# Fused attention on one core: the order of TensorE's work inside a key tile

## The chip, the cores and the metric

The kernel runs on one core of a Trainium2 chip. The metric is the device time of one execution, in microseconds (us). The core has five engines that work side by side: TensorE (PE, with its weight loads PEld), VectorE (DVE), ScalarE (ACT), GpSimd (POOL) and SyncE (SP), which issues DMA transfers. Each runs its own list of instructions in order, and they wait for one another by semaphores.

## The reference

Two transformer layers for 4 batches of 1024 tokens with 128 channels. The change touches the attention of the second layer alone. It has a dense part with 16 heads of 8 channels, and a sparse part with one head of 64 channels that keeps the 204 largest weights of each row. (The sizes written in its first line are not the input's; the token count here is 1024.)

```python
def _L1_attn_ref(src, in_proj_w, in_proj_b, out_proj_w, out_proj_b, Qp_w, Qp_b, Kp_w, Kp_b, Vp_w, Vp_b, lam, ...):
    B, S, D, H, R, DFF = (4, 128, 128, 16, 64, 512)
...
    scores = jnp.einsum('bhqd,bhkd->bhqk', q, k) / math.sqrt(dh)
    attn = jax.nn.softmax(scores, axis=-1)
    ctx = jnp.einsum('bhqk,bhkd->bhqd', attn, v)
    ctx = ctx.transpose(0, 2, 1, 3).reshape(b, s, d)
    dense_output = ctx @ out_proj_w.T + out_proj_b
    Q = src @ Qp_w.T + Qp_b
    K = src @ Kp_w.T + Kp_b
    V = src @ Vp_w.T + Vp_b
    QK = jnp.einsum('bqr,bkr->bqk', Q, K) / math.sqrt(R)
    aw = jax.nn.softmax(QK, axis=-1)
    kk = max(1, int(s * 0.2))
    topv, topi = jax.lax.top_k(aw, kk)
...
    sparse_attn = sparse_attn / (jnp.sum(sparse_attn, axis=-1, keepdims=True) + 1e-09)
    sparse_output = jnp.einsum('bqk,bkd->bqd', sparse_attn, V)
    sig = jax.nn.sigmoid(lam)
    fused = sig * dense_output + (1.0 - sig) * sparse_output
```

## The kernel before

`attend` (from line 2247) computes both parts. It walks over 4 batches, and in each over 4 groups (`GROUPS`), so 16 groups. The dense part of a group is four heads; the sparse part of a group is two tiles of 128 rows (t = 0 and 1). A group has 32 steps (`STEPS`): 8 key tiles of 128 keys, and in each key tile two pairs of heads times two halves of the 1024 queries (`c`). "Key tile" below means four steps, n = 4k to 4k + 3.

Each step n is a score on TensorE (`score`, line 2532): two matmuls, one for each head of the pair, into `scores_ps[n % 2]`. ScalarE then takes the exponential into `probs` (line 2505). There are only two score buffers, so score n waits until exponential n - 2 is done (line 2529). One step's output is 128 x 1024 numbers.

The value products (`values`, line 2549) multiply the exponentials of the key tile before by its values into `pv_ps`: four matmuls of 32 columns for each half c. They are accumulated over the 8 key tiles, and the last key tile's are made in the next group's first steps. Then VectorE copies `pv_ps` to `pv` (`keep_pv`, line 2666, counted by `pv_kept`), and the first product of the next group (`kt == 0`, issued at n = 5) waits for that copy (line 2547).

The side work goes through one buffer, `misc`, whose uses follow one another: `misc_made` counts what TensorE has made, `misc_used` what was taken out. For each group these are: the two sparse scores of this group (`sparse_scores`, line 2569), which VectorE takes out (`keep_scores`, line 2670); and for the previous group the turned output (`turn_out`, 2580), the turned sparse weights (`turn_weights`, 2589), which ScalarE copies out (`keep_turned`, 2482), and the product with the sparse values (`sparse_values`, 2598), for t = 0 and 1. In the kernel before, turn_out, turn_weights and sparse_values are issued in halves of four 128-column blocks, each behind a score of its own.

`PE_AT` and `ACT_AT` say behind which step each piece of side work is issued. On TensorE: sparse scores behind 0 and 4, then the halves in pairs behind 7 and 8, 11 and 12, 15 and 16, 19 and 20, 23 and 24. On ScalarE: `rows_exp` (line 2478, the sparse rows' exponential) behind exponentials 14 and 22, `keep_turned` behind 13 and 21.

VectorE runs one long list for a group (`body`, line 2806): the first sparse score out, the copy of `pv`, the second sparse score out, then the search for the cut of each row, the weights and the outputs. At its end (line 2781) `w_ready` lets TensorE turn the group's weights. At the end of the stage (`end`, line 2648) the last group's side work is done with nothing beside it: eight transposes, both value products in a row, eight transposes.

## Time and profile before

| what | us |
|---|---|
| median of 3 runs | 1391.15 |
| lowest and highest run | 1388.97, 1391.48 |
| the profiled execution | 1388.52 |
| its span in the profile | 1386.8 |
| of that, `attend`, first score to last group's end | 473.8 to 1118.7 |

Busy shares over the span are TensorE 91%, VectorE 75%, ScalarE 66%, GpSimd 40%. They are means over stages with different limits. A row of a group of instructions gives how often it ran, its busy time, the mean length of one, and how long its engine stood idle just before it and for whom. A row of the timeline gives the start, the length, the engine, the line, the operation with its tiles, and how many were merged into it. A duration reaches from the start to the last result, so on ScalarE and TensorE the next instruction can start before the one before has ended; what counts for the pace is the distance of the starts.

### The profile page before, as it was taken

How to read it: one execution, taken by the hardware profiler on the slowest of the kernel's cores; microseconds unless marked ns; L12 is line 12 of the kernel's file. 1: busy time of each engine (PE TensorE's matmuls, PEld its weight loads, DVE VectorE, ACT ScalarE, POOL GpSimd, SP SyncE). 2: the span in 40 equal slices, each digit the busy share in tenths (PEclk: the TensorE clock that was granted, in tenths of full speed). 3: DMA queues.
4: the chain of work that ended last, by engine and by line, in shares of the span. 5: the costliest groups of instructions: out<-in, count | busy, mean ns of one | idle time of the engine just before them, and what ended most of it. 6: DMA issues, size and time to landing. Idle time of an engine off the chain costs nothing. (4 is left out here: it accounts for less than half of the span.)

```text
span 1386.8 us, 28727 instructions
## 1 busy us (share of the span) xinstructions
PE 1266.7 (91%) x9145; PEld 810.6 (58%) x9146; DVE 1041.6 (75%) x2727; ACT 917.3 (66%) x1321; POOL 557.6 (40%) x696
## 2 busy tenths in 40 slices
PE   6999759999986689999999999998999989998999
PEld 4877759999954224443333344333344366878898
DVE  5656267688778688888888788887898858786654
ACT  4565523333356488898888888887888838774232
POOL 6337978867779310222222022222112200488700
PEclk9999779999988899999999999999999989999999
DMA  8980013332335731222221212222122023011211
GB/s 262 224 56 22 31 55 106 98 87 77 93 100 186 200 48 33 40 37 44 41 43 32 35 32 37 44 42 45 21 32 41 3 88 101 19 58 58 70 36 32
DMA packets 100385, 93.96 MB, mean 68 GB/s; under 512 B 20034, under 2 KB 84000, under 8 KB 100256
## 3 DMA queue, kind: packets, MB, share of 16 engines
q1 hardware_dynamic: 92960, 77.51, 25.7%
q0 software_dynamic: 6144, 12.73, 3.0%
q10 hardware_dynamic: 1152, 2.10, 0.5%
q8 instruction: 69, 1.13, 0.4%
q14 instruction: 60, 0.49, 0.2%
HBM read 50.40 MB, written 41.89 MB: 67 GB/s over the span
## 5 line engine op out<-in xcount | busy, mean ns | idle before, releaser
L2505 ACT ACTIVATE probs<-scores_ps 128x1024 f32<-128x1024 f32 x512 | 507.0, 1027 | 89.5 <-PE scores_ps L2532 84.9
L2532 PE MATMUL scores_ps<-q_pack,k_pack 64*128 64x512 f32 x1024 | 245.7, 492 | 37.0 <-ACT probs L2505 21.0
L2532 PEld LDWEIGHTS scores_ps<-q_pack,k_pack 64*128 64x128 f32 x1024 | 96.2, 184 | 310.4 <-issue 163.6
L2549 PE MATMUL pv_ps<-probs,v_pad 128*32 128x512 f32 x2048 | 275.5, 611 | 0.0
L2426 POOL TENSOR_TENSOR squares<-sparse_scores 128x512 f32<-128x512 f32 x32 | 41.0, 1280 | 476.9 <-DVE sparse_scores L2670 476.7
L1447 ACT ACTIVATE hidden_experts<-pre_experts 128x512 f32<-128x512 f32 x94 | 59.3, 631 | 109.5 <-DVE pre_experts L1381 83.1
L2742 DVE TENSOR_SCALAR_CACHE_REDUCE junk<-sparse_scores,at 128x1024 f32<-128x1024 f32 x96 | 122.8, 1279 | 3.4
L1469 PE MATMUL up_ps_experts<-x_t_experts,up_weights_now_experts 128*128 128x128 f32 x752 | 105.2, 284 | 5.5 <-DVE up_weights_now_experts L1376 3.9
L1469 PEld LDWEIGHTS up_ps_experts<-x_t_experts,up_weights_now_experts 128*128 128x128 f32 x752 | 92.6, 194 | 11.0 <-DVE up_weights_now_experts L1376 8.0
L1476 PE MATMUL down_ps_experts<-weights_t,hidden_experts 128*128 x736 | 97.2, 275 | 0.0
L3340 POOL DMA_INDIRECT expert_rows_dram<-expert_input_tail,send_to_tail x64 | 62.5, 977 | 79.5 <-DVE send_to_tail L3468 61.0
L1476 PEld LDWEIGHTS down_ps_experts<-weights_t,hidden_experts 128*128 128x128 f32 x736 | 89.5, 192 | 0.0
L3669 ACT ACTIVATE hidden_tail<-up_ps_tail,weights_t 128x160 f32<-128x160 f32 x128 | 40.9, 393 | 67.0 <-PE up_ps_tail L3808 66.1
L2549 PEld LDWEIGHTS pv_ps<-probs,v_pad 128*32 128x32 f32 x2048 | 40.6, 108 | 64.3 <-issue 62.2
L168 POOL DMA_INDIRECT expert_rows_dram<-expert_input,pick x64 | 64.6, 1009 | 31.0 <-issue 22.9
L1381 DVE TENSOR_TENSOR pre_experts<-up_ps_experts,weights_t 128x512 f32<-128x512 f32 x94 | 64.2, 683 | 16.1 <-PE up_ps_experts L1469 15.2
L2598 PE MATMUL misc_ps<-sparse_v,sparse_w_t 128*128 (+1 forms) x480 | 69.5, 288 | 0.0
L2598 PEld LDWEIGHTS misc_ps<-sparse_v,sparse_w_t 128*128 128x128 f32 x480 | 58.1, 191 | 14.3 <-issue 14.3
L1376 DVE COPY up_weights_now_experts<-weights_t 128x512 f32 x96 | 62.6, 654 | 1.6 <-PEq L462 1.4
L2670 DVE TENSOR_SCALAR_CACHE_REDUCE sparse_scores<-misc_ps 128x1024 f32<-128x1024 f32 x32 | 39.2, 1225 | 26.6 <-PE misc_ps L2569 17.1
L3840 PE MATMUL out_ps_tail<-gated_out_pieces_tail,place_tail 128*128 128x128 bf16 x960 | 56.7, 219 | 0.0
L3840 PEld LDWEIGHTS out_ps_tail<-gated_out_pieces_tail,place_tail 128*128 128x128 bf16 x960 | 55.2, 98 | 0.5
(420 smaller groups left out, 2545.6 us busy)
## 6 DMA issues: line engine op xcount, KB each, us to landing
q_pack<-q_pieces_dram SPq DMA_DIRECT2D x128, 64.0 KB
k_pack<-k_pieces_dram SPq DMA_DIRECT2D x128, 64.0 KB
expert_rows_dram<-zeros SPq DMA_DIRECT2D x1, 6400.0 KB, 22.8
x_rows_experts<-expert_rows_dram SPq DMA_DIRECT2D x25, 256.0 KB
expert_rows_dram<-y_rows_experts SPq DMA_DIRECT2D x46, 128.0 KB, 1.8
q_pieces_dram<-q_pieces_prep SPq DMA_DIRECT2D x8, 512.0 KB, 4.1
k_pieces_dram<-k_pieces_prep SPq DMA_DIRECT2D x8, 512.0 KB, 4.5
expert_rows_dram<-zeros SPq DMA_DIRECT2D x1, 2640.0 KB, 40.2
```

The lines of the kernel that those rows point to most:

```text
L168: pool.indirect_dma_start(self.rows, bass.IndirectOffsetOnAxis(ap=g.pick0[:, b, k, n : n + 1], axis=0), self.h[:, b * NT + n, :], None).th ...
L1376: dve.tensor_copy(up_now[:, k % UNROLL], up_w(e)).then_inc(up_here, 1)
L1381: dve.tensor_tensor(pre[:, k % 2], up_ps[k % 2][:], up_bias(e).unsqueeze(2).to_broadcast([P, FC, P]), ALU.add).then_inc(pre_ready, 1)
L1469: ins = pe.matmul(up_ps[k % 2][:, c, :], up_now[:, k % UNROLL, c, :], x_t[:, k % UNROLL, :], start=True, stop=True)
L1476: ins = pe.matmul(down_ps[k % 2][:, 0:C], hidden[:, k % 2, c, :], down_w(e, c), start=(c == 0), stop=(c == FC - 1))
L2505: act.activation(probs[:, kt % 2, 2 * pair : 2 * pair + 2, c * 512 : c * 512 + 512], scores_ps[n % 2][:].rearrange("p (h t) -> p h t", h=2 ...
L2532: ins = pe.matmul(scores_ps[n % 2][:, head * 512 : head * 512 + 512], k_pack[group % 2][rows, pair, kt * P : kt * P + P].bitcast(F32R), q_ ...
L2549: ins = pe.matmul(pv_ps[32 * j : 32 * j + 32, c, :], v_pad[:, group % 2, kt, j, :], probs[:, kt % 2, j, c * 512 : c * 512 + 512], start=(k ...
L2598: ins = pe.matmul(misc[:, 0:C], w_t[:, n, :], f.sparse_v[:, bass.ds(b * NT + n, 1), :].rearrange("p n c -> p (n c)"), start=(n == 0), stop ...
L2742: step(dve.tensor_scalar(junk[:], s[:, t, :], at[:, t : t + 1], None, ALU.is_ge, ALU.add, accum_out=count[:, t : t + 1]))
L3340: pool.indirect_dma_start(expert_rows.rows, bass.IndirectOffsetOnAxis(ap=send_to[:, b, k, n : n + 1], axis=0), n3[:, b % 3, n, :], None).t ...
L3840: ins = pe.matmul(out_ps[h][:, i * C : i * C + C], place[:, (b * SLOT_TILES + t) % PLACES, n * P : n * P + P], pieces[:, (b * MIX_PARTS + ...
```

## The change

The order inside a key tile is another, and so are the places of the side work. Before, TensorE issued: score, (half a side piece), score, value product 0, score, value product 1, score, (half a side piece). Now it issues: score, score, both value products, score, score, one whole side piece. The whole pieces stand behind steps 3, 7, 11, 15, 19, 23 and 27 of a group. ScalarE's `rows_exp` moves behind exponentials 18 and 26 and `keep_turned` behind 17 and 25. The instructions of each kind, their sizes, their buffers and the lists of VectorE, GpSimd and SyncE stay as they are.

```diff
-PE_AT = (0, 4, 7, 8, 11, 12, 15, 16, 19, 20, 23, 24)
-ACT_AT = (14, 22, 13, 21)
+PE_AT = (3, 7, 11, 15, 19, 23, 27)
+ACT_AT = (18, 26, 17, 25)
...
-                def halves(part):
-                    return range(part * HALF, part * HALF + HALF)
-
-                def turn_out(b, group, number, part):
-                    if part == 0:
-                        free(number)
-                        pe.wait_ge(pv_kept, b * GROUPS + group + 1)
-                    for n in halves(part):
+                def turn_out(b, group, number):
+                    free(number)
+                    pe.wait_ge(pv_kept, b * GROUPS + group + 1)
+                    for n in range(NT):
                         ins = pe.transpose(misc[:, n * P : n * P + P], pv[:, n * P : n * P + P], g.ident[:])
-                    if part == 1:
-                        ins.then_inc(misc_made, 1)
+                    ins.then_inc(misc_made, 1)
...
-                            for part in range(2):
-                                side |= {
-                                    PE_AT[2 + part]: lambda part=part: turn_out(*prev, use(*prev, 2), part),
-                                    PE_AT[4 + part]: lambda part=part: turn_weights(*prev, 0, use(*prev, 3), part),
-                                    PE_AT[6 + part]: lambda part=part: sparse_values(*prev, 0, part),
-                                    PE_AT[8 + part]: lambda part=part: turn_weights(*prev, 1, use(*prev, 5), part),
-                                    PE_AT[10 + part]: lambda part=part: sparse_values(*prev, 1, part),
-                                }
+                            side |= {
+                                PE_AT[2]: lambda: turn_out(*prev, use(*prev, 2)),
+                                PE_AT[3]: lambda: turn_weights(*prev, 0, use(*prev, 3)),
+                                PE_AT[4]: lambda: sparse_values(*prev, 0),
+                                PE_AT[5]: lambda: turn_weights(*prev, 1, use(*prev, 5)),
+                                PE_AT[6]: lambda: sparse_values(*prev, 1),
+                            }
                         for n in range(STEPS):
                             score(b, group, n)
 
-                            if n % 4 in (1, 2):
-                                if n >= 4:
-                                    values(b, group, n // 4 - 1, n % 4 - 1)
-                                elif not alone:
-                                    values(*prev, NT - 1, n % 4 - 1)
+                            if n % 4 == 1:
+                                for c in range(2):
+                                    if n >= 4:
+                                        values(b, group, n // 4 - 1, c)
+                                    elif not alone:
+                                        values(*prev, NT - 1, c)
                             if n in side:
                                 side[n]()
```

`turn_weights` and `sparse_values` change in the same way as `turn_out`, and so does the call of `turn_out` in `end`.

In the order's rows, x counts matmuls: a score is x2, one half's value product x4. Lines of the kernel before are named L2532 (score), L2549 (value product), L2569 (sparse score), L2589 (turned weights); in the changed kernel these are L2531, L2548, L2568 and L2582. TensorE, the start of a group before: the first row is the last score of the group before and score 0, the last row the second sparse score:

```order
-L2532 MATMUL scores_ps<-q_pack,k_pack 128x512 x4
-L2569 MATMUL misc_ps<-sparse_keys_now,sparse_q_tile 128x512 x2
-L2532 MATMUL scores_ps<-q_pack,k_pack 128x512 x2
-L2549 MATMUL pv_ps<-probs,v_pad 32x512 x4
-L2532 MATMUL scores_ps<-q_pack,k_pack 128x512 x2
-L2549 MATMUL pv_ps<-probs,v_pad 32x512 x4
-L2532 MATMUL scores_ps<-q_pack,k_pack 128x512 x4
-L2569 MATMUL misc_ps<-sparse_keys_now,sparse_q_tile 128x512 x2
```

and now, from scores 2 and 3 on:

```order
+L2531 MATMUL scores_ps<-q_pack,k_pack 128x512 x4
+L2568 MATMUL misc_ps<-sparse_keys_now,sparse_q_tile 128x512 x2
+L2531 MATMUL scores_ps<-q_pack,k_pack 128x512 x4
+L2548 MATMUL pv_ps<-probs,v_pad 32x512 x8
+L2531 MATMUL scores_ps<-q_pack,k_pack 128x512 x4
+L2568 MATMUL misc_ps<-sparse_keys_now,sparse_q_tile 128x512 x2
+L2531 MATMUL scores_ps<-q_pack,k_pack 128x512 x4
+L2548 MATMUL pv_ps<-probs,v_pad 32x512 x8
```

Before, four scores and both halves of the last group's product stood between the two sparse scores, and the group's own first product (behind score 5) came only after the second one. Now the last group's product is made ahead of the first row shown, the first sparse score comes behind score 3, and only scores 4 and 5 lie between it and the group's own first product (the x8 row), which waits for the copy of `pv`.

TensorE, a key tile with turned weights, before:

```order
-L2549 MATMUL pv_ps<-probs,v_pad 32x512 x4
-L2532 MATMUL scores_ps<-q_pack,k_pack 128x512 x2
-L2549 MATMUL pv_ps<-probs,v_pad 32x512 x4
-L2532 MATMUL scores_ps<-q_pack,k_pack 128x512 x2
-L2589 MATMUL misc_ps<-ident,sparse_exp 128x128 x4
-L2532 MATMUL scores_ps<-q_pack,k_pack 128x512 x2
-L2589 MATMUL misc_ps<-ident,sparse_exp 128x128 x4
-L2532 MATMUL scores_ps<-q_pack,k_pack 128x512 x2
```

and now:

```order
+L2548 MATMUL pv_ps<-probs,v_pad 32x512 x8
+L2531 MATMUL scores_ps<-q_pack,k_pack 128x512 x4
+L2582 MATMUL misc_ps<-ident,sparse_exp 128x128 x8
+L2531 MATMUL scores_ps<-q_pack,k_pack 128x512 x4
+L2548 MATMUL pv_ps<-probs,v_pad 32x512 x8
```

A score was followed by something else four times in such a tile, and is twice now; the scores stand in pairs.

## Rows read from the trace of the kernel before

**Rows 1.** The page's part 5: busy, mean ns, idle before, and releasers.

```profile
L2505 ACT ACTIVATE probs<-scores_ps 128x1024 f32<-128x1024 f32 x512 | 507.0, 1027 | 89.5 <-PE scores_ps L2532 84.9
L2532 PE MATMUL scores_ps<-q_pack,k_pack 64*128 64x512 f32 x1024 | 245.7, 492 | 37.0 <-ACT probs L2505 21.0 <-PEq L1847 10.0 <-issue 5.3
```

**Rows 2.** Busy time by engine (count) in the last group's window; PEclk, DMA, GB/s.

```profile
1078.05:1117.85 39.80, 38.89 (x258) 15.65 (x256) 34.13 (x78) 35.26 (x38) 9.35 (x9) 1.00 0.02 5
```

**Rows 3.** Timeline of TensorE's weight loads, last group: start us, length us, engine, work.

```profile
1088.82 0.18 PEld L2532 LDWEIGHTS scores_ps<-q_pack,k_pack 64*128 64x128 f32 x2 [0.17 <-issue]
1089.24 0.16 PEld L2549 LDWEIGHTS pv_ps<-probs,v_pad 128*32 128x32 f32 x8 [0.24 <-issue]
1090.24 0.19 PEld L2532 LDWEIGHTS scores_ps<-q_pack,k_pack 64*128 64x128 f32 x2 [0.84 <-ACT probs L2505]
...
1092.09 0.42 PEld L2589 LDWEIGHTS misc_ps<-ident,sparse_exp 128*128 128x128 f32 x4 [0.24 <-issue]
1092.68 0.19 PEld L2532 LDWEIGHTS scores_ps<-q_pack,k_pack 64*128 64x128 f32 x2 [0.17 <-issue]
...
1093.70 0.18 PEld L2532 LDWEIGHTS scores_ps<-q_pack,k_pack 64*128 64x128 f32 x2 [0.17 <-issue]
...
1096.97 0.97 PEld L2598 LDWEIGHTS misc_ps<-sparse_v,sparse_w_t 128*128 128x128 f32 x8 [0.24 <-issue]
1098.06 0.19 PEld L2532 LDWEIGHTS scores_ps<-q_pack,k_pack 64*128 64x128 f32 x2
...
1113.16 0.38 PEld L2532 LDWEIGHTS scores_ps<-q_pack,k_pack 64*128 64x128 f32 x4 [0.84 <-issue]
1114.78 0.19 PEld L2532 LDWEIGHTS scores_ps<-q_pack,k_pack 64*128 64x128 f32 x2 [1.24 <-ACT probs L2505]
...
1117.63 0.19 PEld L2532 LDWEIGHTS scores_ps<-q_pack,k_pack 64*128 64x128 f32 x2 [0.84 <-issue]
1118.71 0.86 PEld L2637 LDWEIGHTS scores_ps<-ident,sparse_exp 128*128 128x128 f32 x8 [0.89 <-ACT probs L2505]
1119.73 0.16 PEld L2549 LDWEIGHTS pv_ps<-probs,v_pad 128*32 128x32 f32 x8 [0.17 <-issue]
...
1121.59 0.86 PEld L2637 LDWEIGHTS scores_ps<-ident,sparse_exp 128*128 128x128 f32 x8 [0.84 <-issue]
```

**Rows 4.** Timeline of ScalarE in the same stretch.

```profile
1096.96 1.16 ACT L2478 ACTIVATE sparse_exp<-sparse_scores,minus_row_max 128x1024 f32<-128x1024 f32 x1
...
1098.10 3.04 ACT L2505 ACTIVATE probs<-scores_ps 128x1024 f32<-128x1024 f32 x3
...
1113.71 2.85 ACT L2505 ACTIVATE probs<-scores_ps 128x1024 f32<-128x1024 f32 x3 [0.41 <-PE scores_ps L2532]
...
1118.17 1.02 ACT L2505 ACTIVATE probs<-scores_ps 128x1024 f32<-128x1024 f32 x1 [0.40 <-PE scores_ps L2532]
```

**Rows 5.** Timeline of all engines at the start of the last group.

```profile
1078.23 0.41 PEld L2569 LDWEIGHTS misc_ps<-sparse_keys_now,sparse_q_tile 64*128 64x128 f32 x4
...
1079.51 1.23 DVE L2670 TENSOR_SCALAR_CACHE_REDUCE sparse_scores<-misc_ps 128x1024 f32<-128x1024 f32 x1 [0.97 <-PE misc_ps L2569]
...
1080.90 0.15 DVE L2673 TENSOR_SCALAR minus_row_max<-row_max 128x1 f32<-128x1 f32 x1 [0.16 <-DVE sparse_scores L2670]
...
1082.48 1.23 DVE L2666 COPY pv<-pv_ps 128x1024 f32<-128x1024 f32 x1 [1.42 <-PE pv_ps L2549]
...
1083.98 1.22 DVE L2670 TENSOR_SCALAR_CACHE_REDUCE sparse_scores<-misc_ps 128x1024 f32<-128x1024 f32 x1 [0.28 <-PE misc_ps L2569]
```

**Rows 6.** Windows in the first group (columns of rows 2), then TensorE's timeline there.

```profile
490.80:494.20 3.40, 1.90 (x16) 0.69 (x14) 3.26 (x7) 3.31 (x5) 0.00 (x0) 1.00 0.68 96
501.10:504.50 3.40, 1.89 (x18) 0.72 (x14) 3.30 (x5) 3.40 (x6) 0.00 (x0) 1.00 0.05 16
504.50:507.90 3.40, 3.40 (x18) 0.49 (x10) 3.29 (x6) 1.84 (x2) 0.00 (x0) 0.50 0.03 7
...
503.55 0.49 PE L2532 MATMUL scores_ps<-q_pack,k_pack 64*128 64x512 f32 x2 [1.51 <-ACT probs L2505]
```

More of the change, by code:

```diff
@@ L2256, in attend @@
     LAST = GROUPS - 1
-    HALF = NT // 2
     LOADS = 2 * (2 * PIECES * PIECES + 1)
@@ L2570, in sparse_scores, with turn_weights, sparse_values @@
                     ins.then_inc(misc_made, 1)
[L2572 to L2597 removed]
+                def turn_out(b, group, number):
+                    free(number)
+                    pe.wait_ge(pv_kept, b * GROUPS + group + 1)
+                    for n in range(NT):
+                        ins = pe.transpose(misc[:, n * P : n * P + P], pv[:, n * P : n * P + P], g.ident[:])
+                    ins.then_inc(misc_made, 1)
+                def turn_weights(b, group, t, number):
+                    free(number)
+                    pe.wait_ge(w_ready, b * GROUPS + group + 1)
+                    for n in range(NT):
+                        ins = pe.transpose(misc[:, n * P : n * P + P], e[:, t, n * P : n * P + P], g.ident[:])
+                    ins.then_inc(misc_made, 1)
+                def sparse_values(b, group, t):
+                    pe.wait_ge(w_t_ready, (b * GROUPS + group) * 2 + t + 1)
+                    for n in range(NT):
                         ins = pe.matmul(
@@ L2604, in sparse_values @@
                         )
-                    if part == 1:
-                        ins.then_inc(misc_made, 1)
+                    ins.then_inc(misc_made, 1)
                 def body(b, first):
@@ L2652, in end @@
                     last_weights(b, 1)
-                    for part in range(2):
-                        turn_out(b, LAST, last_use(2), part)
+                    turn_out(b, LAST, last_use(2))
                     for t in range(2):
```

11 lines of the change are left out of this document (removed).

## The prediction, as it was put on record before the changed kernel ran

> **What bounds the kernel now.** I read the page first, then a window over one group of the fused attention, then the timelines of the weight loads (they mark where TensorE's next piece begins) and of ScalarE in that group. The change touches only `attend`, which runs from 473.8 to 1118.7 us, 16 groups. ScalarE is idle for 89.5 us before its 512 exponentials, nearly always for a score, and TensorE is idle for only 37.0 us before its scores [rows 1]. One group takes 39.8 us with TensorE busy for 38.9 of them, VectorE for 34.1 and ScalarE for 35.3 [rows 2]. So TensorE paces it. In the weight loads the reader is to see a fixed pattern: score to value product 0.42 us, value product to score 1.00, four transposes to score 0.59 [rows 3]. A key tile with half a transpose piece behind two of its scores takes 2 x (0.42 + 1.00) + 2 x (0.42 + 0.59) = 4.86 us and nothing in it waits: from 1088.82 to 1093.70. The sparse product piece has 1.09 per half (1096.97 to 1098.06).
>
> Two chains run behind that, and both have slack now. First, the scores alternate between two buffers, so score n waits for exponential n-2: an exponential that starts at 1113.71 frees the score load at 1114.78, 1.07 us later [rows 3, 4]. A score that loads at 1117.63 starts its exponential at 1118.17, 0.54 us later [rows 3, 4]; three exponentials in a row take 2.85 us where one takes 1.02, so they start 0.91 apart [rows 4]. Second, VectorE copies a finished `pv_ps` out (L2666) only after it has taken the first sparse score (L2670) [rows 5], and the first value product of the next group waits for that copy.
>
> **The change: what it takes off TensorE.** The loads of two scores in a row are 0.19 apart (0.38 us for two scores' loads from 1113.16), against 0.42 when a product follows. Two value products in a row stand once in the trace, in the end of the stage: 1119.73 to 1121.59, 1.86 us, against 2.00 for two halves. Eight transposes in a row take 1.02 (1118.71 to 1119.73), against 1.18 [rows 3]. So a tile needs 2 x (0.19 + 0.42) + 1.86 + 1.02 = 4.10 us of TensorE in place of 4.86. That is the gain. For the sparse product whole, no row stands in this order; it is between 1.94 (twice the 0.97 us of a half's eight loads) and 2.18 (two halves as they stand) [rows 3], and I take 2.0. It is hidden in either case.
>
> **What it puts on the two-buffer chain.** Count from the load of the second score of a tile, s1, at 0. The products start at 0.42 and s2 loads at 0.42 + 1.86 = 2.28. ScalarE started the exponential before s0 at -1.07 (that is what lets s1 load at 0), those of s0 and s1 at -0.16 and 0.75, and is dry from 1.78. Exponential s2 starts at 2.28 + 0.54 = 2.82, exponential s3 at 3.73, and the next tile's s1, which needs the buffer of s3, loads at 3.73 + 1.07 = 4.80. The side piece (from 2.89 to 3.91, or 4.89 for the sparse product) lies wholly beside this. So the period is 4.80 us for a tile with transposes, with nothing or with sparse scores: TensorE's saving is spent waiting. Where ScalarE also does `rows_exp` between the two exponentials (n = 18 and 26), its start-to-start pitch of 1.14 (1096.96 to 1098.10) [rows 4] comes on top: 5.94. `keep_turned` behind n = 17 and 25 is a pass of the shape of an exponential and falls into the dry time before s2: nothing. Group: 6 x 4.80 + 2 x 5.94 = 40.7 us.
>
> **What it puts on the copy of pv.** The first sparse scores move from behind n = 0 to behind n = 3. They load at 2.47 + 0.19 = 2.66. VectorE takes them 1.28 later (1078.23 to 1079.51), its next small operation starts 1.39 after that (1080.90), and I add 0.1 to reach the copy: 5.43 [rows 5]. The copy takes 1.23, and I add 0.1 for the release: 6.76. Today the copy starts late for another reason (it waits for the products behind n = 2, 1082.48) but is followed by a score, sparse scores and a score before n = 5 needs it; after the change only two scores lie between, and the products behind n = 5 would start at 4.80 + 0.42 = 5.22. So they wait 1.5 us, in order, with every later score behind them. The ends for this wait: 0, if VectorE got to the copy before the sparse scores, which the code's order excludes, and 2.0. Group: 40.7 + 1.5 = 42.2, which is 2.4 more than 39.8. The other moved pieces keep their distance: turned output, weights and their keepers all move three or four steps, like VectorE's stream that feeds them. GpSimd's squares and the DMA queue wait for VectorE and for score counts and are not near the path.
>
> **End, start, loops.** The stage ends when VectorE has finished its stream: from its second sparse score at 1083.98 [rows 5] to the transposes at 1118.71 [rows 3] are 34.7 us. Now that score comes 10.3 after s1 of tile 0 (products 6.76, s2 8.62, sparse scores 8.99, plus 1.28), so the last group lasts 0.9 + 10.3 + 34.7 = 45.9 from its first score, in place of 1118.71 - 1078.05 = 40.7: +5.2. For the first group, which has no previous one to work off, I take +1.5 (between 0 and 3: same period, no wait for pv). At the two loop turns the scores lose 5.3 us to issue [rows 1]; about 1 us of each falls into the new wait of the first scores: -2.
>
> Sum without the clock: 14 x 2.4 + 5.2 + 1.5 - 2 = +38.
>
> **The clock.** From 501.1 to 504.5 TensorE was busy 1.89 of 3.40 us, and the granted clock was 0.50 in the next stretch, the 1.2 GHz level; after 490.8 with 1.90 it stayed full [rows 6]. After the change, from the end of the first sparse scores to the products behind n = 5 (about 3.8 to 6.76), TensorE does two scores, 0.8 to 1.0 us in 3.0. That is less busy than the stretch before that fall. I expect a fall in most groups, 13 of 15. At the low level the double product that follows would need up to 1.86 more and the scores some tenths; where the clock falls later, part of the cost lies in waits. Between 0.9 and 2, I take 1.6 per fall: +21. The Trainium skill, "TensorE: Matmul & The Clock Gate", section "HAM oscillation — how this bites in real kernels", says that only idle gaps well above any here have to be avoided. By it no fall would come and the time would be rival B's. The row at 501.1 speaks against it, as its longest gap was 1.51 us [rows 6].
>
> Total +59 us. Profiled execution: 1388.5 + 59 = 1447.5; the median of the runs shown is 2.6 above that execution, so 1450 us.
>
> **Rivals.** B: everything as above, but the clock stays: 1391.15 + 38 = 1429. For it: the fall depends on alignment, and 490.8 had no fall at 1.90 busy. C: the wait for pv doesn't arise or is covered and only the two-buffer chain acts: 14 x 0.9 + 3.7 + 1.5 - 2 = +16, so 1407. Against it: the order of VectorE's list. D, the other side: the exponentials are fed in time, because the pair of products needs less than its one sighting in the end stage, so that the saving on TensorE counts. It decides at a tile period of 4.97 with no wait for pv (39.8 / 8); if it holds fully, TensorE needs 8 x (1.22 + 1.86) and some 9.3 of side work, 34 us a group, and VectorE's stream is next, 1.5 + 1.3 + 34.7 = 37.5: 15 x 2.3 = 34 less, 1357. Against it: the products must stream between s1 and s2 while ScalarE holds at most two scores. E: the clock falls twice in a group, also at the tile without a side piece, where TensorE needs only 3.1 of 4.80: another 13 x 1.6, so 1471. That the change doesn't do what it says is excluded by the order: pairs of scores, eight products, whole pieces.
>
> **Numbers.** Forecast A 0.53, B 0.20, E 0.09, C 0.09, D 0.06, unplaced 0.03. Range 1424 to 1466: A and B with the bounds of the fall's price. A measurement of this kernel tells about 0.2% from no change. Faster by over 0.2%: 0.06; within: 0.03; slower: 0.91.
>
> **What would show it.** Right: groups of about 42 to 44 us; score loads in pairs 0.19 apart; a period of 4.80 in quiet tiles and 5.94 in the two with `rows_exp`; ScalarE idle for a score about 1.0 us before every n = 2 mod 4; TensorE waiting for L2666's copy, 1.5 us a group; a granted clock of 0.50 for a stretch in most groups. Wrong: TensorE without waits for exponentials behind the pairs (D), no wait for the copy (C), clock 1.00 throughout (B). My weakest term is the clock, then the double product, seen once.

## The result

The changed kernel is slower. Its median is 1464.49 us (4 runs, 1460.33 to 1470.27) against 1391.32 us of the kernel before (4 runs, 1388.97 to 1391.54): a ratio of 1.054, with a 95% interval of 1.0515 to 1.0565. The forecast was 1450 us, 59 us more than before. The medians differ by 73. The direction came as forecast and the size was too small. The mechanism came as forecast in the plain groups, and not in the first group and at the loop turns.

The profiled execution is the longest of its four (1470.27 us, span 1468.5). Against the one of before it is 81.7 us longer, so the accounts below, which are made from these two, hold some 8 us more than the medians do.

The lines that answer to [rows 1], from the page's part 5 of the changed kernel (busy, mean ns, idle before, and releasers):

```profile
L2504 ACT ACTIVATE probs<-scores_ps 128x1024 f32<-128x1024 f32 x512 | 486.4, 1028 | 178.4 <-PE scores_ps L2531 174.6
L2531 PE MATMUL scores_ps<-q_pack,k_pack 64*128 64x512 f32 x1024 | 226.6, 481 | 87.2 <-ACT probs L2504 72.7
L2548 PE MATMUL pv_ps<-probs,v_pad 128*32 128x512 f32 x2048 | 277.2, 663 | 28.2 <-DVE pv L2654 25.4
L2658 DVE TENSOR_SCALAR_CACHE_REDUCE sparse_scores<-misc_ps 128x1024 f32<-128x1024 f32 x32 | 39.2, 1225 | 117.1 <-PE misc_ps L2568 103.8
```

The same list shows VectorE idle before the sparse scores for 103.8 us, since TensorE now makes them later. ScalarE's idle time for a score went from 84.9 to 174.6 us, and TensorE's idle time for an exponential from 21.0 to 72.7. Each now waits for the other, in turns. A third wait is new: 25.4 us in which TensorE's products wait for VectorE's copy of `pv`.

Busy time by engine (PE, PEld, DVE, ACT, POOL), granted clock, DMA share and GB/s of two groups, as in [rows 2]: first one in which the clock fell, then one in which it stayed.

```profile
1104.11:1148.11 44.00, 38.23 (x256) 16.25 (x257) 34.51 (x81) 34.25 (x39) 7.34 (x9) 0.96 0.23 34
880.73:923.08 42.35, 36.60 (x256) 15.82 (x256) 35.06 (x82) 34.24 (x39) 7.34 (x9) 1.00 0.24 35
```

At full clock TensorE is busy for 36.6 us in a group, 2.3 less than the 38.9 of before. So the work on TensorE did shrink as meant. But the group takes 42.35 us in place of 39.80.

**A quiet tile.** The weight loads of TensorE, as in [rows 3], in a key tile with turned weights behind it and in the one that follows:

```profile
897.66 0.19 PEld L2531 LDWEIGHTS scores_ps<-q_pack,k_pack 64*128 64x128 f32 x2 [0.66 <-ACT probs L2504]
898.09 0.16 PEld L2548 LDWEIGHTS pv_ps<-probs,v_pad 128*32 128x32 f32 x8 [0.24 <-issue]
...
899.94 0.30 PEld L2531 LDWEIGHTS scores_ps<-q_pack,k_pack 64*128 64x128 f32 x4 [0.84 <-ACT probs L2504]
900.60 0.85 PEld L2582 LDWEIGHTS misc_ps<-ident,sparse_exp 128*128 128x128 f32 x8 [0.36 <-issue]
901.62 0.19 PEld L2531 LDWEIGHTS scores_ps<-q_pack,k_pack 64*128 64x128 f32 x2 [0.17 <-ACT probs L2504]
902.47 0.19 PEld L2531 LDWEIGHTS scores_ps<-q_pack,k_pack 64*128 64x128 f32 x2 [0.66 <-ACT probs L2504]
...
908.42 0.18 PEld L2531 LDWEIGHTS scores_ps<-q_pack,k_pack 64*128 64x128 f32 x2 [0.83 <-ACT probs L2504]
```

From the second score of one tile to that of the next are 4.81 us (897.66 to 902.47), and 5.95 to the next (908.42), in whose middle `rows_exp` stands. The double product holds the next pair of scores for 1.85 us after its own load at 898.09. ScalarE in the same tile:

```profile
895.67 3.77 ACT L2504 ACTIVATE probs<-scores_ps 128x1024 f32<-128x1024 f32 x4 [1.05 <-PE scores_ps L2531]
900.48 1.02 ACT L2504 ACTIVATE probs<-scores_ps 128x1024 f32<-128x1024 f32 x1 [1.04 <-PE scores_ps L2531]
```

It does four exponentials in a row, 3.77 us, then has nothing for 1.04 us. That is the chain of the prediction: two buffers hold two scores, and the third can't come before both products are through.

**The copy of pv.** All engines at the start of a group, as in [rows 5]:

```profile
884.27 0.43 PEld L2568 LDWEIGHTS misc_ps<-sparse_keys_now,sparse_q_tile 64*128 64x128 f32 x4
...
885.58 1.23 DVE L2658 TENSOR_SCALAR_CACHE_REDUCE sparse_scores<-misc_ps 128x1024 f32<-128x1024 f32 x1 [0.94 <-PE misc_ps L2568]
...
886.46 0.19 PEld L2531 LDWEIGHTS scores_ps<-q_pack,k_pack 64*128 64x128 f32 x2 [0.73 <-ACT probs L2504]
...
887.08 1.23 DVE L2654 COPY pv<-pv_ps 128x1024 f32<-128x1024 f32 x1
...
888.46 1.92 PE L2548 MATMUL pv_ps<-probs,v_pad 128*32 128x512 f32 x16 [1.49 <-DVE pv L2654]
```

The products could have started 0.42 us after the load of score 5 at 886.46. They start at 888.46. VectorE first took the late sparse score out (885.58), then copied `pv` (887.08), and TensorE stood for 1.49 us.

**The clock.** Windows in the same columns, first two in the first group, which answer to [rows 6], then two around the start of another plain group (at 742.08), then three around the start of the last but one group (at 1104.11), and TensorE's timeline there:

```profile
501.30:504.70 3.40, 1.01 (x6) 0.37 (x4) 3.33 (x6) 3.35 (x5) 0.00 (x0) 1.00 0.53 65
504.70:508.10 3.40, 3.40 (x18) 0.59 (x16) 3.30 (x5) 1.54 (x2) 0.00 (x0) 0.50 0.03 9
740.20:743.60 3.40, 2.10 (x16) 0.83 (x16) 3.26 (x7) 2.60 (x3) 0.00 (x0) 1.00 0.26 61
743.60:747.00 3.40, 3.40 (x18) 0.57 (x10) 1.68 (x7) 1.17 (x2) 0.00 (x0) 0.50 0.51 69
1102.00:1105.40 3.40, 2.10 (x16) 0.67 (x8) 3.29 (x6) 2.37 (x3) 0.00 (x0) 1.00 0.26 65
1108.80:1112.20 3.40, 1.46 (x10) 0.56 (x12) 2.58 (x4) 2.82 (x4) 1.85 (x2) 1.00 0.55 65
1112.20:1115.60 3.40, 3.40 (x18) 1.03 (x12) 0.00 (x0) 0.00 (x0) 1.98 (x4) 0.51 0.57 83
```

```profile
1109.84 0.50 PE L2531 MATMUL scores_ps<-q_pack,k_pack 64*128 64x512 f32 x2 [0.42 <-ACT probs L2504]
1111.84 3.29 PE L2548 MATMUL pv_ps<-probs,v_pad 128*32 128x512 f32 x16 [1.49 <-DVE pv L2654]
1115.05 1.00 PE L2531 MATMUL scores_ps<-q_pack,k_pack 64*128 64x512 f32 x4
...
1118.28 1.92 PE L2548 MATMUL pv_ps<-probs,v_pad 128*32 128x512 f32 x16
```

In the stretch that holds the wait for `pv` TensorE was busy for 1.46 of 3.40 us; the granted clock of the next stretch is 0.51, the 1.2 GHz level. The double product that falls into it takes 3.29 us, and the next one, at full clock, 1.92. The falls come at two places. In five of the ten plain groups the fall comes at this wait for `pv`. In three it comes earlier, 1.4 to 1.6 us after the group's first score, behind a tile without a side piece: the stretch before 743.60 has 2.10 us of work and no gap above 0.9 us, and the next one ran at 0.50. The stretch from 1102.00 has 2.10 us of work too, and no fall behind it.

From the first score of `attend` to its last, TensorE's clock fell 20 times, where it had fallen 3 times before. One more fall, at 1194.2, comes between the last score and the end of the last group.

**Where the 81.7 us are.** The length of a group is from its first score's load to that of the next group.

| stretch | before | after | difference | forecast |
|---|---|---|---|---|
| up to the first score of `attend` | 473.8 | 475.4 | +1.6 | 0 |
| first group | 38.9 | 48.6 | +9.7 | +1.5 |
| ten plain groups | 397.7 | 436.5 | +38.9 | +38 to +40 |
| four groups beside the two loop turns | 167.7 | 187.6 | +19.9 | some +14 |
| last group, to the transposes | 40.7 | 47.6 | +6.9 | +5.2 |
| after `attend` | 268.1 | 272.8 | +4.7 | 0 |

Of the ten plain groups, two took 42.20 and 42.36 us without a fall of the clock, and eight took 43.93 to 44.04 with one. The eight tiles of a group took 4.82, 7.19, 4.89, 4.82, 5.78, 4.99, 5.78 and 4.92 us (first score to first score, medians of the ten plain groups).

### The profile page after: what moved, and what is told of

Same layout as the page of the kernel before. It is cut to its first block and busy times, and to the rows that moved or that the text cites. A ratio compares the mean times of both kernels' runs of the same rounds, so it can differ in the third digit from the quotient of the medians.

```text
span 1468.5 us, 28727 instructions
## 1 busy us (share of the span) xinstructions
PE 1264.3 (86%) x9145; PEld 819.3 (56%) x9146; DVE 1044.2 (71%) x2727; ACT 901.0 (61%) x1321; POOL 551.8 (38%) x696
## 5 line engine op out<-in xcount | busy, mean ns | idle before, releaser
L2504 ACT ACTIVATE probs<-scores_ps 128x1024 f32<-128x1024 f32 x512 | 486.4, 1028 | 178.4 <-PE scores_ps L2531 174.6
L2531 PE MATMUL scores_ps<-q_pack,k_pack 64*128 64x512 f32 x1024 | 226.6, 481 | 87.2 <-ACT probs L2504 72.7
L2548 PE MATMUL pv_ps<-probs,v_pad 128*32 128x512 f32 x2048 | 277.2, 663 | 28.2 <-DVE pv L2654 25.4
L2531 PEld LDWEIGHTS scores_ps<-q_pack,k_pack 64*128 64x128 f32 x1024 | 88.3, 189 | 296.0 <-ACT probs L2504 235.7
L2425 POOL TENSOR_TENSOR squares<-sparse_scores 128x512 f32<-128x512 f32 x32 | 40.8, 1274 | 552.5 <-DVE sparse_scores L2658 552.5
L2548 PEld LDWEIGHTS pv_ps<-probs,v_pad 128*32 128x32 f32 x2048 | 58.3, 115 | 148.6 <-issue 125.6
L2658 DVE TENSOR_SCALAR_CACHE_REDUCE sparse_scores<-misc_ps 128x1024 f32<-128x1024 f32 x32 | 39.2, 1225 | 117.1 <-PE misc_ps L2568 103.8
L3657 ACT ACTIVATE hidden_tail<-up_ps_tail,weights_t 128x160 f32<-128x160 f32 x128 | 40.8, 393 | 69.8 <-PE up_ps_tail L3796 68.6
L2588 PE MATMUL misc_ps<-sparse_v,sparse_w_t 128*128 (+1 forms) x480 | 61.5, 281 | 0.0
```

What stands on the lines that cost most here:

```text
L2504: act.activation(probs[:, kt % 2, 2 * pair : 2 * pair + 2, c * 512 : c * 512 + 512], scores_ps[n % 2][:].rearrange("p (h t) -> p h t", h=2 ...
L2531: ins = pe.matmul(scores_ps[n % 2][:, head * 512 : head * 512 + 512], k_pack[group % 2][rows, pair, kt * P : kt * P + P].bitcast(F32R), q_ ...
L2548: ins = pe.matmul(pv_ps[32 * j : 32 * j + 32, c, :], v_pad[:, group % 2, kt, j, :], probs[:, kt % 2, j, c * 512 : c * 512 + 512], start=(k ...
L2588: ins = pe.matmul(misc[:, 0:C], w_t[:, n, :], f.sparse_v[:, bass.ds(b * NT + n, 1), :].rearrange("p n c -> p (n c)"), start=(n == 0), stop ...
```

## The experiments

In the table "plain group" is the length of most groups of the stage, and "falls" counts, in the one profiled execution, how often the granted clock fell to its lower level between the first and the last score of `attend`. The ratios are to the kernel before as it ran in the same session. Its medians there were 1389.2 to 1391.3, so a plain difference of two medians can be some 2 us off.

| kernel | median us | ratio to before (95%) | plain group | falls |
|---|---|---|---|---|
| before | 1391.3 | | 39.8 | 3 |
| changed | 1464.5 | 1.054 (1.0515 to 1.0565) | 42.2 or 44.0 | 20 |
| e3: before, products paired | 1423.3 | 1.0242 (1.0225 to 1.0259) | 41.4 | 6 |
| e2: changed, products apart | 1442.3 | 1.0389 (1.0371 to 1.0406) | 41.8 | 8 |
| e1: changed, sparse scores early | 1428.9 | 1.028 (1.0256 to 1.0304) | 41.2 | 8 |
| e12: changed, copy of pv first | 1427.1 | 1.0242 (1.0207 to 1.0278) | 40.8 | 6 |
| e5: changed, scores repeated | 1447.1 | 1.0414 (1.0389 to 1.044) | 42.4 | 4 |
| e6: e5, more in the first group | 1445.4 | 1.0396 (1.038 to 1.0411) | 42.4 | 3 |
| e13: changed, no loops | 1448.6 | 1.0425 (1.0387 to 1.0463) | 42.3 or 43.9 | 12 |
| e9: changed, `rows_exp` later | 1480.0 | 1.0647 (1.0632 to 1.0663) | 43.0 to 45.2 | 18 |
| e4: whole side pieces | 1385.9 | 0.9978 (0.9966 to 0.9991) | 39.2 to 39.6 | 3 |
| e7: one side piece in each tile | 1414.7 | 1.0161 (1.0136 to 1.0187) | 40.2 to 42.4 | 7 |
| e10: e7, `rows_exp` behind 18 and 23 | 1387.0 | 0.9972 (0.9956 to 0.9988) | 39.6 | 2 |
| e11: e7, `rows_exp` behind 14 and 22 | 1378.8 | 0.9914 (0.9892 to 0.9936) | 39.0 | 3 |
| e14: e11, no loops | 1368.2 | 0.9843 (0.9818 to 0.9869) | 39.0 | 0 |

### Pairing alone

e3 is the kernel before with one edit: both value products stand behind the second score.

```diff
-                            if n % 4 in (1, 2):
-                                if n >= 4:
-                                    values(b, group, n // 4 - 1, n % 4 - 1)
-                                elif not alone:
-                                    values(*prev, NT - 1, n % 4 - 1)
+                            if n % 4 == 1:
+                                for c in range(2):
+                                    if n >= 4:
+                                        values(b, group, n // 4 - 1, c)
+                                    elif not alone:
+                                        values(*prev, NT - 1, c)
```

> The kernel before with one edit: both value products behind n = 1 mod 4. Side work stays in halves and sparse scores behind 0 and 4. Theory: the two-buffer chain alone acts. Tiles take 4.8 to 4.9 us (before: 4.47 to 5.4, with only the slow ones bound by TensorE), those with rows_exp 5.9, a group about 41.4 in place of 39.8, total about 1417 us, with few falls of the clock. Rival (TensorE's pace counts, and the pairing saves it 0.14 on the products and 0.23 on the scores of a tile): about 8 x 0.37 x 16 = 47 us less, down to 1345 us, or VectorE's bound at 1357 us.

Measured: 1423.34 us, 34 us more than before in the same session (1389.17). A plain group without a fall takes 41.43, with tiles of 4.8 to 5.1 and two of 5.81. The chain of the two buffers holds, and needs nothing else of the change. The rival that pairing saves time falls.

e2 is the other way round, the changed kernel with the products apart again (the same lines, + and - exchanged).

> The changed kernel with its value products apart again, behind n = 1 and 2 mod 4; sparse scores and whole side pieces stay where the change put them. Theory: the last score of a tile now loads 2.84 us after the second, the next tile's second one at 2.84 + 0.54 + 1.07 = 4.45 in place of 4.80, so quiet tiles take 4.45 to 4.5 us and those with rows_exp about 5.7. The wait for the copy of pv grows to about 2.2, as the double product no longer covers part of it. Group about 40.4 without a fall, 42 with one; total about 1435 us. Rival (no two-buffer chain, the wait for pv and the clock make the whole loss): tiles as before at best, loss at least as large, 1465 us or more.

Measured: 1442.27 us. The direction is right, but the group is 1.4 us longer than expected: 41.77. From second score to second score a quiet tile takes 4.46 or 4.47. Eight of these are 35.8. Of the 6.0 above, 2.2 come with the wait for `pv`, which is still there (the step of the product behind score 5 takes 3.66 us where others take 1.42 to 1.53), and twice 1.8 with the tiles in which `rows_exp` and a whole side piece stand beside each other (6.31 each).

### The copy of pv

Two experiments take that wait away, on different engines. e1 moves the two sparse scores on TensorE:

```diff
-PE_AT = (3, 7, 11, 15, 19, 23, 27)
+PE_AT = (0, 4, 11, 15, 19, 23, 27)
```

> The changed kernel with its two sparse scores back behind steps 0 and 4; pairs, double products and all other whole pieces stay. My theory (three terms: two-buffer chain, wait for the copy of pv, clock): the wait before the products of step 5 goes, since VectorE can copy pv about 1.5 us before they are due. The sparse scores now stand between the two scores of a pair and cost about 0.35 us each: 40.7 + 0.7 = 41.4 us a group in place of the 42.2 of the groups of the changed kernel without a fall. If the falls of the clock come from that wait they mostly go too, and the time is about 1425 us; if they come from the whole pattern they stay at 1.8 a group, 1450 us. Rival (the double products alone make the time, the wait for pv only takes up time that is idle anyway): no less than 1460 us.

Measured: 1428.85 us, groups of 41.17 and 8 falls of the clock in place of 20, near the 41.4 and 1425 that were expected. The rival, that the wait only takes up idle time, falls.

e12 leaves TensorE's list as it is and exchanges two entries of VectorE's:

```diff
+                        if prev:
+                            keep_pv(step, *prev)
                         keep_scores(step, b, group, 0)
...
-                        if prev:
-                            keep_pv(step, *prev)
```

> The changed kernel with one edit in VectorE's list: the copy of pv stands ahead of the first sparse score, not behind it. TensorE's and ScalarE's lists are the changed kernel's. The wait before the products of step 5 alone is taken away. Theory: step 5 takes 2.3 us as in the other tiles, a group 40.7 to 41.0, the falls of the clock go with the wait outside the first group, total 1415 to 1425 us. Rival (the falls come from the pairs and gaps of all tiles): step 5 at 2.3 but groups of 42.5 with falls elsewhere, 1440 us.

Measured: 1427.14 us, 37 less than the changed kernel. One group in e12, and the copy, now ahead of the sparse scores, with the product that it had delayed:

```profile
1074.40:1115.19 40.79, 36.52 (x256) 15.71 (x256) 34.56 (x81) 34.23 (x39) 7.36 (x9) 1.00 0.24 37
```

```profile
1077.71 1.22 DVE L2654 COPY pv<-pv_ps 128x1024 f32<-128x1024 f32 x1
...
1080.10 0.49 PE L2531 MATMUL scores_ps<-q_pack,k_pack 64*128 64x512 f32 x2 [0.41 <-ACT probs L2504]
...
1080.53 1.92 PE L2548 MATMUL pv_ps<-probs,v_pad 128*32 128x512 f32 x16
```

The product starts 0.43 us after its score. The plain group is 40.8, which the prediction had worked out as 40.7 for the two-buffer chain alone. The ten plain groups together lose 23.1 us and `attend` has 14 falls of the clock fewer. So the wait for `pv` costs 2.3 us a plain group: 1.4 by itself (42.2 to 40.8) and 0.9 through the clock. Two of its ten plain groups still have a fall (42.40 and 42.42 us), both at the group's start, where the copy plays no part, and a third (43.11) begins in a low stretch that it takes over from the first group. The two groups ahead of the loop turns gain 3.2 and 2.9 us (42.5 and 42.9), and the two behind them hardly gain (48.4 and 46.9).

### The clock

e5 makes four scores of a group four times over (the matmuls are repeated with the same result), around the places where TensorE has too little to do:

```diff
+WARM = (0, 4, 5, 31)
...
-                    for head in range(2):
+                    for head in (0, 1) * (4 if n in WARM else 1):
```

> The changed kernel with the two matmuls of the scores of steps 0, 4, 5 and 31 made four times each, into the same buffer: the same result, 0.64 us more of TensorE in places where it waits (steps 0, 5 and 31 have 0.5 to 1.5 us of waiting behind them). Theory (the clock falls because TensorE has too little to do there, and each fall costs about 1.8 us): most falls outside the first group vanish, groups of 44.0 become 42.2 to 42.4, total about 1440 us. Rival (the longer steps 1 and 5 are not the clock's, or more work costs its own time): the time stays at 1464 us or grows by up to 16 x 2 us.

Measured: 1447.06 us, 7 more than expected. One group in it:

```profile
1086.00:1128.40 42.40, 38.83 (x281) 17.84 (x280) 34.49 (x81) 34.53 (x39) 7.37 (x9) 1.00 0.19 36
```

TensorE does 24 matmuls more in each group and the kernel is 17 us faster. The waits stay (the step of the product behind score 5 still takes 3.84 us), the falls go from 20 to 4, and all ten plain groups take 42.34 to 42.43. With the same waits and more work, a group that had taken 44.0 takes 42.4, so the 1.6 between them are the clock. That is the term of the prediction, seen by itself. The repeated scores stand at both places of the falls, so e5 doesn't tell these apart; e12 does.

e6 adds the same for steps 0 and 3 of every tile in the first group (the repeated scores again give the same result).

```diff
-                    for head in (0, 1) * (4 if n in WARM else 1):
+                    first_group = isinstance(b, int) and b == 0 and group == 0
+                    for head in (0, 1) * (4 if n in WARM or (first_group and n % 4 in (0, 3)) else 1):
```

> As the kernel with four times repeated scores at steps 0, 4, 5 and 31, and in the first group also at every step with n mod 4 of 0 and 3, where no side work stands. Theory (the first group took 48.6 us in place of 38.9 mostly because the clock fell five times in it): the first group comes down to 41 to 43 us, total 6 us below that kernel, about 1434 us. Rival (the first group is long through the two-buffer chain and its start): no gain over that kernel, or a loss.

Measured: 1445.43 us, and a first group of 45.6 us, where 41 to 43 was expected and e5 has 46.3. As a whole this missed. But the falls of the first group are gone: it had five in the changed kernel, two in e5 and none here (the three falls of e6 lie around the loop turns). Its last six tiles in e6, and the same tiles in the changed kernel (same columns as above):

```profile
488.51:520.10 31.59, 28.69 (x220) 12.90 (x217) 27.10 (x55) 25.35 (x29) 3.53 (x4) 1.00 0.30 43
484.72:523.98 39.26, 29.16 (x144) 7.69 (x145) 30.27 (x58) 25.02 (x29) 5.00 (x7) 0.78 0.25 35
```

They take 7.7 us less at full clock. The first two tiles take 13.97 us in place of 9.29, which eats 4.7 of it. The stage begins at the low clock (0.67 granted in these two tiles of e6), and repeated scores cost there before they bring anything.

### The loop turns

In the changed kernel two groups behind a loop's jump stand out. VectorE there, and TensorE:

```profile
833.82 0.17 DVE L2769 RECIPROCAL w_sum<-w_sum 128x2 f32<-128x2 f32 x1
841.17 1.23 DVE L2658 TENSOR_SCALAR_CACHE_REDUCE sparse_scores<-misc_ps 128x1024 f32<-128x1024 f32 x1 [7.19 <-issue]
...
842.71 1.23 DVE L2654 COPY pv<-pv_ps 128x1024 f32<-128x1024 f32 x1
```

```profile
844.08 3.64 PE L2548 MATMUL pv_ps<-probs,v_pad 128*32 128x512 f32 x16 [5.05 <-DVE pv L2654]
```

The same place in the kernel before:

```profile
792.09 0.17 DVE L2781 RECIPROCAL w_sum<-w_sum 128x2 f32<-128x2 f32 x1
796.99 1.23 DVE L2670 TENSOR_SCALAR_CACHE_REDUCE sparse_scores<-misc_ps 128x1024 f32<-128x1024 f32 x1 [4.73 <-issue]
```

VectorE needs 4.73 us before and 7.19 after from its last instruction of one round to the first of the next (4.77 and 6.12 at the other turn), with no wait that the profile shows. Not all of it need be the jump's. In groups behind no jump VectorE stands at this place too, for the sparse score: 0.7 to 1.0 us before, and in the changed kernel 3.2 to 3.4 where the clock fell at the group's start, as it did behind both jumps. Less these, the jump adds 3.8 and 3.9 us before, and 3.9 and 2.8 after. Before, no product stood behind that. Now TensorE waits 5.05 us for it. e13 writes the four batches out on every engine, with no loop in `attend` (the count of `misc` uses and GpSimd's list change with it):

```diff
...
-            body(0, True)
-            with eng.Fori(1, B) as b:
-                body(b, False)
+            for b in range(B):
+                body(b, b == 0)
...
```

> The changed kernel with the four batches of the stage written out on every engine, in place of one body and a loop over three. The instructions and their order are the same, only the two jumps back go. The four groups around the loop turns took 19.9 us more than in the kernel before (187.6 against 167.7), where my sum had 14 for them. Theory (the jumps delay VectorE's first sparse score by some 7 us, and TensorE now waits for the copy behind it): all groups 42.2 to 44.0, 12 us less in all, about 1452 us. Rival (the turn of a batch costs this through its transfers or buffers): no less than 1462 us.

Measured: 1448.61 us. The four groups that lie beside the turns took 45.74, 48.89, 45.75 and 47.23 us and now take 43.89, 43.93, 43.87 and 43.90, like any other group with a fall of the clock. VectorE at that place:

```profile
823.83 0.17 DVE L2766 RECIPROCAL w_sum<-w_sum 128x2 f32<-128x2 f32 x1
827.26 1.22 DVE L2655 TENSOR_SCALAR_CACHE_REDUCE sparse_scores<-misc_ps 128x1024 f32<-128x1024 f32 x1 [3.27 <-PE misc_ps L2565]
```

It waits for the sparse score and no longer for itself. The loop, with the jumps of all engines together, was the cause of 12.0 us. In the kernel before, the same four groups take 8.7 us more than four plain ones (167.7 against 4 x 39.77). The first group came down too, from 48.55 to 42.57, which I had not expected: the clock fell once in it and not five times.

### What limits the other orders

e9 puts `rows_exp` on ScalarE behind the products, where ScalarE has nothing to do:

```diff
-ACT_AT = (18, 26, 17, 25)
+ACT_AT = (21, 29, 17, 25)
```

> The changed kernel with rows_exp behind exponentials 21 and 29, where ScalarE is dry before the next score, in place of 18 and 26. Theory of the two-buffer chain alone: the two tiles of 5.8 come down to 5.0, a group to 40.5 without a fall, total about 1440 us. But VectorE closes a loop of its own: first sparse score, copy of pv (2.8), double product and two score loads and the second sparse score (3.5), its list to the end (34.7), 41.0, and rows_exp for the second rows comes about 1 us late for it: 42.0 us, hardly less than 42.2. I expect the second: total 1450 to 1465 us. A time of 1440 or less would say that VectorE has slack.

Measured: 1480.01 us, where 1450 to 1465 was expected: a miss as a whole and a hit in its part. The pairs of tiles around `rows_exp` took 5.78 + 4.99 and 5.78 + 4.92 us and now take 5.78 + 4.65 and 5.84 + 4.65, so the dry time of ScalarE does take a part of the pass. But VectorE needs its result. The waits of e9 between 513 and 1120 us (total, times, longest):

```profile
PE pv_ps L2548 <- DVE pv L2654: 42.8, 14, 9.0
DVE junk L2740 <- ACT sparse_exp L2477: 40.4, 14, 4.6
```

VectorE waits 2.9 us a group for `rows_exp`, and TensorE's wait for the copy of `pv` is 42.8 us in place of 25.4. That VectorE hands its delay on through the copy is my reading of the two; no run separates them.

e4, e7, e10 and e11 keep the whole side pieces of the change and put the products apart, as before. e4 has `PE_AT = (0, 4, 7, 11, 15, 19, 23)` and `ACT_AT = (14, 22, 13, 21)`.

> The kernel before with one edit: side pieces whole, behind steps 7, 11, 15, 19 and 23; value products apart, sparse scores behind 0 and 4, ScalarE's pieces behind 14, 22, 13 and 21. Theory: TensorE saves 0.16 and a switch of scores in a tile with transposes (4.86 to about 4.47) and meets the two-buffer chain there at 4.45, 5.7 in the two tiles with rows_exp; a group takes 38.1 to 38.5 us, total about 1369 us. VectorE's list (37.5 us a group) is next. Rival (a whole piece starves ScalarE as a double product does, since it also keeps the next score from loading): tiles of 4.9 us or more and 1391 us or more.

Measured: 1385.86 us, groups of 39.6 at most. The expectation was 17 us too low: the second tile carries both a sparse score and the turned output and takes 5.71 us, and a tile with `rows_exp` 5.54 with 5.21 behind it. e7 has at most one side piece in a tile:

```diff
-PE_AT = (3, 7, 11, 15, 19, 23, 27)
-ACT_AT = (18, 26, 17, 25)
+PE_AT = (0, 4, 8, 12, 16, 20, 24)
+ACT_AT = (18, 26, 13, 21)
```

> Value products apart (behind n = 1 and 2 mod 4), whole side pieces, one to a key tile: behind steps 0, 4, 8, 12, 16, 20 and 24; keep_turned behind 13 and 21, rows_exp behind 18 and 26. Theory: the kernel with whole pieces at 7, 11, 15, 19 and 23 missed its 38.3 us a group since its tile 1 had both a sparse score and the turned output (5.7 us of TensorE), while tile 6 had nothing and still took 4.0. Spread out, tiles take 4.45 (sparse), 4.5 (turned) and 5.45 (sparse product, with rows_exp beside it): 37.7, and VectorE's list of 37.5 is next, so 38.0 us a group, total about 1364 us. Rival (VectorE's list binds already at 39.5 in the one before, through its own waits): 1386 us again.

Measured: 1414.7 us, where 1364 was expected. VectorE's wait for `rows_exp` is 39.3 us, 15 times 2.6, as in e9. e10 and e11 differ from e7 in `ACT_AT` alone, (18, 23, 13, 21) and (14, 22, 13, 21).

> The kernel with one whole side piece to a tile, behind steps 0, 4, ... 24, with the second rows_exp behind exponential 23 in place of 26. In that kernel VectorE's weighing of the second rows waited 39.3 us in all for rows_exp, 2.6 a group, which stretched its list from 37.5 to about 40.3, the group's length. Theory: the wait goes, a group takes 38.2 us, total 1366 to 1372 us. Rival (the whole pieces behind the first score of a tile delay the exponentials and set 40.3 by themselves): 1400 us or more, as there.

> The same side pieces on TensorE (behind 0, 4, ... 24), with rows_exp behind 14 and 22 as in the kernel before. rows_exp now falls into the tiles with turned weights and keep_turned, not beside the long sparse products: 5.7 in two tiles and 5.45 in two others, a group of 39.3 to 39.7, total about 1385 us. If it comes out below the one with 18 and 23, VectorE's list and not ScalarE's load is what counts here.

Measured: 1387.01 us for e10, with 39.6 a group. VectorE's wait for `rows_exp` is down to 0.3 us in all and the kernel is 28 us faster than e7, so that wait was what held e7 back in the main. But 38.2 a group and 1366 to 1372 us were expected, and this missed: the sixth tile takes 5.70 us, where e11, whose `rows_exp` stands elsewhere, takes 5.09. e11 came out at 1378.84 us, 6 below what was expected, with 39.0 a group, in which TensorE is busy for 37.5:

```profile
1029.40:1068.40 39.00, 37.52 (x258) 15.51 (x258) 34.57 (x81) 34.90 (x38) 7.36 (x9) 1.00 0.25 38
```

So the whole side pieces are the half of the change that gains, if the products stay apart: 0.2 to 0.5 us a group in e4, and 0.8 in e11, which also spreads them one to a tile. e14 is e11 with the batches written out, as in e13.

> The kernel with value products apart, whole side pieces behind 0, 4, ... 24 and rows_exp behind 14 and 22, with the four batches written out likewise. Its four groups around the loop turns took 166.2 us where four others take 156.0: if the jumps are the cause, 10 us less, about 1369 us; the same if the transfers are.

Measured: 1368.18 us (5 runs), 0.9843 of before. The groups behind the first take 38.95 to 38.99, but for the last with 39.96, and the clock doesn't fall once in `attend`. Against e11 the four groups beside the turns lose 10.3 us, and the medians differ by 10.7. This is the version to keep: 21 us faster than before in the same session (1389.21), and 96 faster than the changed kernel.

## Why the prediction was right or wrong

**The saving on TensorE**: right, and worth nothing, as said. TensorE's busy time in a group without a fall went from 38.9 to 36.6.

**The two-buffer chain**: right. 4.80 was worked out for a quiet tile and 4.81 measured, and 5.94 for a tile with `rows_exp`, against 5.95 (902.47 to 908.42). The group without the wait for `pv` is 40.8 (e12) against 40.7. e3 shows that pairing alone costs 34 us.

**The copy of pv**: right. 1.5 was worked out and 1.49 measured. 42.2 for the group, and 42.20 and 42.36 in the two that kept the clock. Rival C, without this wait, has no support: e12 had to change VectorE's list to make it true.

**The clock**: right in kind, number and price, and in place only in part. 13 of the 15 groups behind the first have a fall, as I had taken. A plain group pays 1.7 for it (43.93 to 44.04 against 42.2 to 42.4) where 1.6 was taken, and e5 shows that apart from the waits. But I had put every fall into the wait for `pv`, and of the eight falls in plain groups three came at the group's start, behind the tile without a side piece. That is the place of rival E, which I had priced as a second fall and not as another place for the one. That the count came out as forecast is in this part luck. e12 takes the wait away, and no fall is left at step 5 in a plain group. The Trainium skill, "TensorE: Matmul & The Clock Gate", section "HAM oscillation — how this bites in real kernels", asks only for long idle gaps to be avoided. By it the time would have been rival B's 1429; here the clock fell with 1.49 us as the longest gap in the stretch ahead, and the measurement decides. B's groups exist, but only two of them.

**The first group**: this is the first step that failed. I took +1.5 from its missing predecessor and counted no fall there, and it was +9.7. With none of a previous group's side work, TensorE had 1.01 of 3.40 us to do at 501.3, and the clock fell five times; steps 13, 17, 21, 25 and 29 took 3.6 to 3.9 us each in place of 2.3, together 7.7. e6, without a fall in these tiles, takes 7.7 us less for them. That is the mechanism of rival E (a fall at tiles without a side piece), in the one group in which six of eight tiles are such tiles. I had weighed E for the plain groups alone, and the row of before on which my clock argument rested, [rows 6], lay in this very group.

**The loop turns**: the second step that failed. I took -2, for issue time that would fall into the new wait. The four groups around the turns came 19.9 us longer. By my own terms (4 x 2.4, 4 x 1.6, -2) that should have been 14. I had asked what a jump does to TensorE and not what it does to VectorE, on whose copy TensorE now hangs. e13 shows what the jumps cost here: 12.0 us, where the kernel before loses 8.7 in these groups. So the turns lose some 3 us more than before, and I had taken 2 less.

**The last group**: +6.9 against +5.2. The sum of its parts had no fall of the clock in it, and there is one at its start; with 1.6 for it the sum gives 6.8. A second fall comes 1.5 us before its end.

**Outside `attend`**: +6.3, which I had put at nothing. Of that, 4.7 lie behind `attend`, whose code the change leaves alone. TensorE's wait of 4.5 us at the end of the last group leaves it a low clock to start with, where the same stretch before ran at 1.00:

```profile
1195.70:1200.00 4.30, 4.27 (x20) 2.16 (x24) 3.20 (x10) 1.02 (x1) 0.00 (x0) 0.50 0.02 4
```

How much of the 4.7 this makes wasn't measured by itself. The other runs point the same way: from the end of `attend` on, those that enter at full clock take 267.2 to 271.7 us, and those that enter with 6.8 us or more of low clock take 272.6 to 273.0, but for e7 with 269.8. e12 enters with the last 3.0 us of a fall and takes 268.0. The 1.6 ahead of `attend` are no more than the runs differ by: the first score comes at 473.1 to 476.0 us in kernels whose work ahead of it is the same.

The terms that failed add up: 8.2 for the first group, some 6 for the turns, 1.7 for the last and 6.3 outside, together 22, and 59 + 22 is 81, where the two profiled executions differ by 81.7. The upper end of the range, 1466, does not follow from what the prediction names for it: 13 falls at 2.0 us instead of 1.6 bring 1450 to 1455, below the 1464.49 measured. **Rival D**, faster, falls: TensorE's wait for exponentials more than tripled.

**Open.** What VectorE's restart behind the jump consists of. By the difference above it is 2.8 to 3.9 us in both kernels, but at the first turn of e12, where the copy stands first and no late sparse score is ahead of it, VectorE stands 8.29 us. Why the clock falls five times in the first group of the changed kernel and once in that of e13, with the same order. And which of the stretches with little work keep the clock: two groups with the same order and the same wait for `pv` had no fall.

## What to carry to other kernels

Where two engines hand work to each other through two buffers, as TensorE and ScalarE here, the longest piece on the producer's list between two fills sets the period, not the sum of its work: keep pieces short there, and lump together only what stands outside the chain. Before a step is moved later, ask who waits for the instruction that stands behind its consumer, here a copy behind the sparse score on VectorE, and try to exchange the two in the consumer's list first. A wait on TensorE is to be priced with the clock that it may cost, and that in every part of the loop on its own, the first round and the jump included, since those have other work beside them.

## What the runs showed of the hardware

- The clock can fall without any long gap: 0.51 granted behind a stretch with 1.46 of 3.40 us busy and 1.49 us idle in one piece, and 0.50 behind one with 2.10 of 3.40 busy, at 743.6. After another with 2.10 of 3.40 busy, from 1102.0, it stayed at 1.00.
- Adding work can shorten a kernel: 24 matmuls more in each group, 17 us less.
- At a jump back in a loop VectorE stands 4.7 to 7.2 us between its last and its next instruction in the kernel before and in the changed one (8.29 in e12, 9.0 in e9), where a part can be the wait for the sparse score. Written out, e14's median is 10.7 us below e11's.
- ScalarE's exponentials of 128 x 1024 last 1.03 us each but follow each other every 0.91 (four in 3.77 us).
